# Splitting the dense expert weights before the first mixer, and making the routed tokens' slots in two halves

## What is computed

```python
xn = layernorm(x)
# the first mixer: a short convolution, linear attention with prefix sums, a gate
q, k, v = split(x1 @ w_qkv.T)              # x1 = xn + conv(xn) @ w_pw.T, 16 heads of 8
num, den = q_phi . cumsum(k_phi * v), q_phi . cumsum(k_phi)
x2 = x1 + sigmoid(delta @ w_gate.T + b_gate) * (num / (den + 1e-6)) @ w_o.T
# four dense experts on every token, weighted by a softmax gate
h  = layernorm(x2) * ln_g + ln_b
s  = x2 + sum_e gw[:, e] * (silu(h @ w1[e].T + b1[e]) @ w2[e].T + b2[e])
# sixteen routed experts on xn, top 1, each with room for 160 tokens
top1_val, top1_idx = max(softmax(xn @ Wg)), argmax
vals, idx = top_k(where(top1_idx == n, top1_val, -inf), 160)     # for each expert n
y[idx] = gelu(xn[idx] @ W1[n] + be1[n]) @ W2[n] + be2[n]          # other tokens keep xn
x  = x + s * silu(y)
# second layer: relative causal attention with 16 heads of 64, and a small feed-forward
```

## Time and profile before

| what | value |
|---|---|
| median of 3 runs | 1211.15 us (1209.11 to 1211.19) |
| profiled execution | 1211.67 us |
| its span | 1209.9 us |
| TensorE busy | 1143.2 us, 94% of the span |
| VectorE busy | 825.1 us, 68% |
| ScalarE busy | 686.0 us, 57% |
| GpSimd busy | 839.1 us, 69% |

### The profile page before, as it was taken

How to read it: one execution, slowest core, us unless ns; L and a number is a source line. 1 busy time by engine, 2 the same in 40 slices (tenths; PEclk the granted TensorE clock), 3 DMA queues, 4 the chain that set the end, 5 groups by cost and what they waited for, 6 DMA issues and landing times.

```text
span 1209.9 us, 31474 instructions
## 1 busy us (share of the span) xinstructions
PE 1143.2 (94%) x11948; PEld 755.6 (62%) x11948; DVE 825.1 (68%) x2036; ACT 686.0 (57%) x1375; POOL 839.1 (69%) x1109
## 2 busy tenths in 40 slices
PE   4899689989988999999999999999999999999997
PEld 2354456668755567666766666666676666676665
DVE  3778978813585886686687678668757867866552
ACT  2534254347424566666666656666666665665665
POOL 0778530050625788888798797888879879788895
PEclk9999899999989999999999999999999999999998
DMA  8300020022113401302132030230203204023001
GB/s 314 128 1 1 1 79 2 1 79 79 36 43 71 110 16 32 85 14 46 33 67 46 15 80 7 45 81 19 46 19 80 45 2 89 11 45 72 10 3 37
DMA packets 74891, 60.19 MB, mean 50 GB/s; under 512 B 38962, under 2 KB 69298, under 8 KB 73652
## 3 DMA queue, kind: packets, MB, share of 16 engines
q1 hardware_dynamic: 73716, 56.08, 18.7%
q0 software_dynamic: 1024, 2.09, 0.6%
HBM read 19.76 MB, written 4.72 MB: 20 GB/s over the span
## 4 chain that ended last, share of the span: by engine, by line
PE 67%; ACT 2%; DVE 1%; issue 1%; DVEq 0%
PE S L1962 10%; PE S L1963 10%; PE S L1964 10%; PE A L1952 9%; PE O L1976 6%; PE O L1977 5%; PE O L1974 5%; PE M L1943 3%; PE M L1920 2%; PE M L1922 2%; PE M L1921 2%; PE M L1937 1%; PE M L1930 1%; PE M L1928 1%; PE M L1929 1%
## 5 line engine op out<-in xcount | busy, mean ns | idle before, releaser
L1704 POOL TENSOR_TENSOR plow<-prob 128x512 f16<-128x512 f32 (+3 forms) x640 | 588.8, 931 | 94.4 <-ACT prob L2180 70.6
L2180 ACT ACTIVATE prob<-S,keep_sigma 128x512 f32<-128x512 f32 (+3 forms) x640 | 395.7, 625 | 265.0 <-PE S L1964 262.0
L2281 DVE CUSTOM_DVE_ANT_0 junk<-A,mask_rows,part 128x512 bf16<-128x512 f32 (+3 forms) x384 | 249.0, 649 | 98.3 <-PE A L1952 77.2
L1974 PE MATMUL O<-V,prob 128*128 128x65 f16 x2176 | 232.7, 193 | 0.2 <-POOL plow L1704 0.2
L1976 PE MATMUL O<-V,prob 128*128 128x64 f16 x2176 | 232.6, 195 | 0.0
L1977 PE MATMUL O<-V,plow 128*128 128x65 f16 x2176 | 231.7, 192 | 0.0
L1962 PE MATMUL S<-rows 97*128 97x512 f16 (+3 forms) x640 | 223.3, 349 | 3.7 <-ACT prob L2180 3.4
L1963 PE MATMUL S<-rows 96*128 96x512 f16 (+3 forms) x640 | 222.5, 348 | 0.0
L1952 PE MATMUL A<-rows 96*128 96x512 f16 (+3 forms) x640 | 221.2, 346 | 1.3 <-DVE part L2281 1.0
L1964 PE MATMUL S<-rows 96*128 96x512 f16 (+3 forms) x640 | 220.9, 345 | 0.0
L1974 PEld LDWEIGHTS O<-V,prob 128*128 128x128 bf16 x2176 | 203.0, 97 | 23.6 <-POOL plow L1704 0.3
(11 more groups left out here) (390 smaller groups left out, 1913.5 us busy)
## 6 DMA issues: line engine op xcount, KB each, us to landing
rows<-stage_rows SPq DMA_DIRECT2D x64, 256.0 KB, 3.4
V<-stage_v SPq DMA_DIRECT2D x16, 516.0 KB, 4.6
W<-in_W SPq DMA_DIRECT2D x2, 2048.0 KB, 15.7
shifted<-turned SPq DMA_DIRECT2D x32, 128.0 KB, 2.3
rows<-stage_pos SPq DMA_DIRECT2D x64, 64.0 KB, 3.1
w<-in_w SPq DMA_DIRECT2D x2, 1024.0 KB, 9.0
xe_rows<-zero SPq DMA_DIRECT2D x1, 1280.0 KB, 5.3
ye_rows<-xe SPq DMA_DIRECT2D x5, 256.0 KB, 2.7
```

The lines of the kernel that those rows point to most:

```text
L1704: pool.tensor_tensor(plow[:, k % PB, 0:w], full, full.bitcast(BF16).rearrange("p (q e) -> p q e", e=2)[:, :, 1], ALU.subtract).then_inc(s_ ...
L1974: pe.matmul(both, high[:, cs, 1], vh[h][:, j, 0:HS + 1], start=(j == 0 and s == 0), stop=False, skip_group_check=True)
L2180: act.activation(prob[:, k % PB, 0:w], S[k % 2][:, 0:w], ACT.Exp, scale=sigma[:, 2 * p + h:2 * p + h + 1]).then_inc(s_exp, 1)
L2281: dve.tensor_tensor_reduce(junk[:, g % 2, 0:w], A[g % 2][:, 0:w], add, -1.0, before, ALU.add, ALU.min, out).then_inc(s_max, 1)
```

## The change

There are three edits.

- **The split of w1 is moved to the first beats of `mixer0`.** w1, ln_g and ln_b (`FIRST_EXPERTS`) are loaded right behind the mixer's own tables, and no longer among the later weights. VectorE runs `bound_parts` before its first beat, TensorE sums it in beat -9 and VectorE makes the scales in beat -8 (`bound_scales`). ScalarE makes both the high halves and the scaled w1 in beat -8, VectorE the low halves in beat -4, GpSimd three small products in beat -4.
- **GpSimd's start of `experts0`.** It waits for eight h tiles before it splits hT, and clears its two tiles behind the four chunks.
- **Slots in halves.** VectorE makes the slots of the first eight tiles after 32 units of counts, and those of the last eight at the end; GpSimd sends eight tiles after each. Two of its steps no longer wait for the one before.

The diff, cut to its core:

```diff
-LATER = ("wg", "rank_order", "ln_g", "ln_b", "w_mg", "w1", "b1", "w2", "b2", "below", "W1", "W2", "be1", "be2")
+FIRST_EXPERTS = ("w1", "ln_g", "ln_b")
+LATER = ("wg", "rank_order", "w_mg", "b1", "w2", "b2", "below", "W1", "W2", "be1", "be2")
...
+            for name in FIRST_EXPERTS:
+                sp.dma_start(t0[name][:], dram[name]).then_inc(s_w1, 16)
...
-                elif u == UNITS - 1:
+                elif u == -SC:
                     bounds_summed()
...
-                elif u == UNITS + 1:
+                elif u == 1 - SC:
                     act.wait_ge(s_ln, 2)
-                    act.activation(w1_high, w1_all, ACT.Copy, scale=scales[:, 0:1]).then_inc(s_sqrt, 1)
+                    act.activation(w1_high, w1_all, ACT.Copy, scale=scales[:, 0:1])
+                    act.activation(w1_all, w1_all, ACT.Copy, scale=scales[:, 0:1]).then_inc(s_sqrt, 1)
...
+                if u == 5 - SC:
+                    pool.wait_ge(s_ln, 2)
+                    for k, v in ((2, t0["ln_g"]), (3, t0["ln_b"])):
+                        pool.tensor_scalar(scales[:, k:k + 1], v[:], scales[:, 1:2], None, ALU.mult)
+                    pool.tensor_tensor(scales[:, 4:5], tops[:, 0:1], tops[:, 1:2], ALU.mult)
             at_beats(beat)
-            pool.wait_ge(s_sqrt, 2)
-            pool.tensor_scalar(w1_all, w1_all, scales[:, 0:1], None, ALU.mult).then_inc(s_scaled, 1)
-            pool.wait_ge(s_scaled, 1)
-            pool.tensor_tensor(w1_low, w1_all, w1_high, ALU.subtract)
...
+                if m == 5 and c == 0:
+                    dve.wait_ge(s_sqrt, 2)
+                    dve.tensor_tensor(w1_low, w1_all, w1_high, ALU.subtract)
...
+            def bound_scales():
+
+                dve.wait_ge(s_rl, 1)
+                step(dve.tensor_scalar(tops[:, 0:2], BOUND, 1e-30, None, ALU.max))
+                dve.reciprocal(scales[:, 0:2], tops[:, 0:2]).then_inc(s_ln, 1)
...
-                if u == UNITS - 2:
-                    bound_parts()
+                if u == 1 - SC:
+                    bound_scales()
...
         def _(pool):
+            pool.wait_ge(s_hn, 2 * TPC)
             for c in range(NC):
...
-                if c == 0:
-                    pool.memset(gwT, 0.0)
-                    pool.memset(zero[:], 0.0).then_inc(s_zero, 1)
+            pool.memset(gwT, 0.0)
+            pool.memset(zero[:], 0.0).then_inc(s_zero, 1)
...
-            pool.wait_ge(s_slot, 1)
             for i in range(NT):
+                if i % HALF == 0:
+                    pool.wait_ge(s_slot, i // HALF + 1)
                 pool.indirect_dma_start(dram["xe_rows"], bass.IndirectOffsetOnAxis(slot[:, i:i + 1], 0), xn_tok[:, i, :], None,
...
-                if unit[0] == len(UNITS):
-                    slots()
+                if unit[0] == HALF * NC:
+                    slots(slice(0, HALF))
+                elif unit[0] == len(UNITS):
+                    slots(slice(HALF, NT))
```

More of the change, by code:

```diff
@@ L397, in sums @@
                     if c == NC - 1:
-                        pe.wait_ge(s_rd, 4)
+                        pe.wait_ge(s_rd, 3)
                     for i in range(TPC):
@@ L408, in route_logits @@
                 for i in range(NT):
-                    pe.matmul(L[:, i * RE:(i + 1) * RE], xnT[:, 2 + i * P:2 + (i + 1) * P], wg[:], start=True, stop=True)
+                    ins = pe.matmul(L[:, i * RE:(i + 1) * RE], xnT[:, 2 + i * P:2 + (i + 1) * P], wg[:], start=True, stop=True)
+                ins.then_inc(s_rl, 1)
             def bounds_summed():
@@ L644, in prefix, with bound_parts @@
                                        ALU.add).then_inc(s_cum, 1)
+            def bound_parts():
+                dve.wait_ge(s_w1, 16 * len(FIRST_EXPERTS))
+                dve.tensor_reduce(parts[:, 0:1], w1_all, AX_X, ALU.max, apply_absolute_value=True)
+                step(dve.tensor_scalar(tops[:, 0:1], t0["ln_g"][:], X_NORM, None, ALU.mult))
+                dve.scalar_tensor_tensor(tops[:, 0:1], t0["ln_g"][:], -X_NORM, tops[:, 0:1], ALU.mult, ALU.max)
+                step(dve.scalar_tensor_tensor(tops[:, 1:2], t0["ln_b"][:], -1.0, t0["ln_b"][:], ALU.mult, ALU.max))
+                step(dve.tensor_tensor(parts[:, 1:2], tops[:, 0:1], tops[:, 1:2], ALU.add))
+                dve.tensor_scalar(parts[:, 0:2], parts[:, 0:2], H_UNIT, None, ALU.mult).then_inc(s_rd, 1)
+            def bound_scales():
+                dve.wait_ge(s_rl, 1)
+                step(dve.tensor_scalar(tops[:, 0:2], BOUND, 1e-30, None, ALU.max))
+                dve.reciprocal(scales[:, 0:2], tops[:, 0:2]).then_inc(s_ln, 1)
             dve.memset(U[:, 0:1], 1.0).then_inc(s_unit, 1)
@@ L883, in experts0 @@
         ROUTED_AT = 10
+        HALF = NT // 2
         block = ctx.enter_context(nc.Block())
@@ L1284, in count_rows, with slots @@
                 unit[0] += 1
-                if unit[0] == len(UNITS):
-                    slots()
-            def slots():
-                dve.wait_ge(s_rc, len(UNITS))
-                step(dve.tensor_reduce(rank[:], counts[:], AX_X, ALU.add))
-                step(dve.tensor_scalar(over[:], rank[:], float(CAP) - 0.5, float(2 * SLOT_ROWS), ALU.is_ge, ALU.mult))
-                step(dve.tensor_scalar(slotf[:], cmax[:], -float(CAP), float(CAP * RE), ALU.mult, ALU.add))
-                step(dve.tensor_tensor(slotf[:], slotf[:], rank[:], ALU.add))
-                step(dve.tensor_tensor(slotf[:], slotf[:], over[:], ALU.add))
-                dve.tensor_copy(slot[:], slotf[:]).then_inc(s_slot, 1)
+                if unit[0] == HALF * NC:
+                    slots(slice(0, HALF))
+                elif unit[0] == len(UNITS):
+                    slots(slice(HALF, NT))
+            def slots(at):
+                dve.wait_ge(s_rc, at.stop * NC)
+                dve.tensor_reduce(rank[:, at], counts[:, at, :], AX_X, ALU.add)
+                step(dve.tensor_scalar(slotf[:, at], cmax[:, at], -float(CAP), float(CAP * RE), ALU.mult, ALU.add))
+                dve.tensor_tensor(slotf[:, at], slotf[:, at], rank[:, at], ALU.add)
+                step(dve.tensor_scalar(over[:, at], rank[:, at], float(CAP) - 0.5, float(2 * SLOT_ROWS), ALU.is_ge, ALU.mult))
+                step(dve.tensor_tensor(slotf[:, at], slotf[:, at], over[:, at], ALU.add))
+                dve.tensor_copy(slot[:, at], slotf[:, at]).then_inc(s_slot, 1)
             def route_counts(k):
```

22 lines of the change are left out of this document (5 added, 17 removed).

## The result

The changed kernel takes 1200.72 us, median of 4 runs (1196.33 to 1202.13), where the kernel before, run beside it, takes 1210.88 (4 runs, 1209.11 to 1211.19): a ratio of 0.9913, 95% interval 0.9885 to 0.9941. So it is faster by 10.2 us where 16.2 were forecast, and 1200.72 lies 1.7 us above the range. The profiled execution was the quickest of the four: 1196.33 us (span 1194.6), against 1211.67 before, and 1195.5 had been forecast for a profiled one. The ratios leave out one run that stood far off, of 1696.67 us at a granted clock of 0.655, in the first experiment (e12). The document has to explain two things: where the 15.3 us of that execution come from, and why the others took 4 to 6 us more than it.

What follows compares the result with a forecast made beforehand. GpSimd's split of w1, holding VectorE's casts in the first mixer's tail, was taken as the main bound. Terms +0.3 - 11.2 - 1.1 - 1.2 + 1.0 - 4.0 = -16.2 us gave a median of 1195.0 us, range 1191.5 to 1199.

Steps and rivals of the forecast that it cites:

- The tail: End of the first mixer: without GpSimd's split, VectorE's casts shorten and TensorE's clock holds; 11.2 us less.
- Rival 4: Mixer's tail: the casts are slow for another reason, so 8.5 + 1.7 us stay, 1205 us; chance 0.02.
- The experts' start: GpSimd held back there: first dense product 1.1 us earlier, and 1.2 us less because the clock holds.
- rival 1: The clock doesn't hold at the experts' start: 1196.2 us, or 1197.3 with the 1.1 lost too; chance 0.15.
- The slots in halves: Routed experts' sends: added slots cost 1.0 us; no wait for returned tokens and a better clock save 4.0 us.
- rival 3: Sends and rank counts exclude one another: eight sends stop VectorE for 7.8 us, 1202.8 us; chance 0.04.
- The start: First beats of the mixer, with the split moved there: 0.3 us more, from 0 to 2, covered by ScalarE's gap.
- Rival 2: At the start w1 lands 2 to 4 us later, sharing engines with later loads: 1197 to 1199 us; chance 0.10.
- Rival 5: Loads share DMA engines evenly, w1 lands at 39.7 us: slower, 1213.4 to 1214 us; chance 0.01.
- the step from the profiled execution to the median: Whole kernel: 1195.5 us for a profiled execution, 0.5 lower for the median, 1195.0.

Runs made afterwards that it cites:

- e12: The changed kernel plus two dead GpSimd passes of 2048 columns at the end of mixer0, against the kernel before: 1211.44 us, ratio 0.9996.
- e3: The kernel before with only the split of w1 moved to the first beats, chip C: 1225.94 us, ratio 0.9932 to the kernel before.
- e4: The changed kernel without the slots in halves, chip C: 1224.35 us, ratio 0.9920 to the kernel before.
- e9: The changed kernel as it is, run again on chip A: 1198.98 us, ratio 0.9904 to the kernel before.
- e10: The changed kernel with ln_g and ln_b loaded ahead of w1, chip A: 1198.76 us, ratio 0.9893 to the kernel before.
- e11: Changed kernel, vectors ahead of w1, bound in beats -1 to 3, ScalarE's passes in pieces, low halves in beat 15, chip A: 1196.60 us, ratio 0.9886 to before.
- e7: Changed kernel, vectors ahead of w1, bound in beats -1 to 3, ScalarE's passes in pieces, low halves in beat 34, chip D: 1221.11 us, ratio 0.9899 to before.
- e14: The changed kernel with one set of slots and sixteen sends in a row, chip E: ratio 0.9917 to the kernel before.

## Why the forecast was right, and where it was wrong

**The tail** (11.2 us, 10.2 of them behind the last scan): 10.25 measured, and of the other 1.0 us, 0.9 (the last scan is 108.7 us behind the first tap for 109.6 before, in the trace whose start cost nothing). From the last scan to the experts it is 25.6 to 25.8 us in every trace with the old split or with the dead passes, and 15.46 to 15.48 in nine with the new one; in the four where the clock had fallen near 130 us already it is 15.7 to 16.5. Both halves of the term, the casts and the clock behind the gap, were right, and e12 shows the cause. Rival 4 falls.

**The experts' start** (1.1, and 1.2 by the clock): 1.28 to the first product, and the clock held in every trace of the change, so rival 1 falls. e3 against e4 gives 0.9 for the second part; the rest of the 1.28 lies with the first.

**The slots in halves** (+1.0 - 4.0 = -3.0): 3.0 by traces on B. The added steps take 0.97 us on VectorE, and the counts beside the first eight sends take 0.75 us as before, so rival 3 falls. The size of the wait's and the clock's share was off by a few tenths each way. On the chips with stalls no gain can be told from nothing, and TensorE has no wait for the tokens there with either kernel, which the trace before could not show.

**The start is the step that failed.** The forecast said +0.3 us, "from 0 to 2", with w1 landed at about 21.5 and the vectors by 22.2, 2.9 us behind the tables, worked out from one 512 KB transfer's 1.1 us. In the first trace they were there at 23.43, 2.95 us behind tables that were late themselves, and the relu moved by 0.03 us against its tap: that this trace came out near the forecast, 1196.33 for 1195.5, is in part luck. In the other eleven the loads were there 3.5 to 5.8 us behind the first tap, at 23.6 to 25.1 us, and the relu moved by 0.2 to 4.2 us. Rival 2 names the landing, with 2 to 4 us, but had 0.10 of the chance and 1199 as its far end; its reason, that w1 shares engines with what is issued behind it, no run tests. The forecast passed over two things. It noted that the bound's product stands ahead of K on TensorE, and took that for covered since K waits anyway; once it isn't, an idle TensorE is behind it, and K's eight products take 1.4 to 2.4 us more at a clock that has fallen. And it took the subtraction to fit into VectorE's time ahead of phi; with it there, GpSimd's addition can come before phi, which is 1.0 us late for it in seven of the twelve traces. (Up to 1 us was named there for the addition meeting the subtraction; the meeting that TensorE pays for is the one with phi.) Rival 5 (all loads sharing evenly, a landing at 39) falls.

The second mistake is in the step from the profiled execution to the median. The forecast took the median 0.5 us under a profiled one, as before the change, but the profiled one of the changed kernel was its quickest of four, by 3.8 us. That the three others were late at the start is an inference from their size and from their clock of 0.991 to 0.993 against 0.995; they have no trace. On A two traced executions, of 1198.27 and 1201.53 us, are late in this way, e9 by the held phi and e10 by both waits. The start doesn't account for all of the spread: the kernel before spread over 2.1 us in its 4 runs on the first chip, but over 8.1 in 13 on A. What it costs in the median is estimated where it is taken out: on A the change gains 12.4 us and e11 14.8, with the overlap said above.

**Open.** What makes the engines stand still in the dense experts on C, D and E. TensorE's longer waits there lie 52 and 92 us behind the first dense product in all seven traces with the slots in halves, and 85 to 87 us behind it in the four without (with a second at 98 to 100 in three), so the place goes with the program and not with the chip alone. They account for 8.5 of the 22 us by which D is slower than B with the kernel before; the rest lies nearly all behind ye (929.4 us for 915.9). And why the clock fell near 130 us in e7, e9, e10 and e14: the last stop of TensorE before it that the trace shows is one of 0.9 us, 12 to 13 us earlier, and the same stop stands in the traces whose clock held. That e11 beats the quickest executions of the change isn't shown (1195.96 us for 1196.33, not timed side by side). The 0.5 us behind ye in the first table were not followed.

## What to carry to other kernels

Work that nobody waits for can still be the most expensive work in a stretch: look for short operations that end when a long one on GpSimd ends, and move the long one, not the short. When work is moved to the start of a program, what it waits for are loads in flight, whose landing varies by microseconds; look also for what it will meet on the engine beside it; put it where the first chain of TensorE doesn't stand behind it (e11), and forecast the median from the spread and not from one trace. And a wait removed at one place is worth something only where no other delay covers it: the same edit gave 2.2 us on one chip and nothing that could be told on three others.

## What the runs showed of the hardware

- A one-column GpSimd operation with two inputs took 2.22 us beside VectorE's subtraction over 2048 columns (31.91 to 34.19) and ended with it, where the same instruction had taken 0.18 in the kernel before; its neighbours of one input took 0.30 and 0.27 just ahead. That cost nothing, since nobody waited for the small product. Just behind it phi and GpSimd's next addition (L549) met: where phi began first the addition took 1.75 for 1.27, and where the addition began first phi took 1.65 to 1.75 for 0.69, in seven traces, which TensorE waited for. The Trainium skill (SBUF — State Buffer, "SBUF: two separate sides") has the port pair of the two engines locked for a whole instruction, by whichever starts first, between a VectorE operation with two SBUF inputs and a GpSimd one that reads SBUF. The traces agree.
- The landing of the same loads differs by nearly 2 us between executions: the first tap began at 18.8 to 20.7 us, the reduce of w1, where it waited for the loads, at 23.4 to 25.1, and 2.9 to 5.8 us behind the tap.
- TensorE's clock was 1.00 from 25 to 35 us in the five traces in which it had stood idle for 0 to 1.24 us ahead of the bound's product, and fell in the seven with 2.39 to 3.50 us. Behind the next wait of 2.71 to 2.85 us it fell in six traces of seven and held in e9; and it fell near 130 us in four traces with no stop of over 1 us in the 12 us before.
- Five chips gave two levels of time for one kernel, 1211 us on two and 1234 on three, with a part of the difference in stops of several engines, at places that moved when the program did.
